# Both masked attentions in the turned form, with a quad's values in three pieces

## The reference, cut to what matters

```python
x = x + L0_xattn(layernorm(x), ctx, ctx, mask0, ...)      # first attention, masked
x = x + L0_ffn(layernorm(x), ...)                         # its weights are quantised to -1, 0, 1
...
x = x + L3_xattn(layernorm(x), ctx, ctx, mask3, ...)      # fourth layer's attention, masked
x = x + L3_ffn(layernorm(x), ...)

# L0_xattn and L3_xattn, B = 4, 16 heads of 8, 256 queries, 1601 keys
q, k, v = heads(Q @ Wq.T + bq), heads(K @ Wk.T + bk), heads(V @ Wv.T + bv)
scores = q @ k.T / sqrt(8)
scores = scores + mask0 * -1e9                  # L0: float mask, 1 is masked
scores = where(mask3 == 0, -1e9, scores)        # L3: int mask, 0 is masked
out = (softmax(scores) @ v).reshape(...) @ Wo.T + bo
```

## Time and profile before

| | before |
|---|---|
| median of three runs | 2109.28 us (2107.88 to 2111.71) |
| the profiled execution | 2111.81 us |
| its span, first to last instruction | 2110.0 us |
| mean granted clock of TensorE | 0.941 |
| TensorE matmuls | busy 1899.7 us, 90% |
| TensorE weight loads | busy 1336.2 us, 63% |
| VectorE | busy 1334.4 us, 63% |
| ScalarE | busy 1297.4 us, 61% |
| GpSimd | busy 309.7 us, 15% |
| DMA | 87.69 MB, mean 42 GB/s |

### The profile page before, as it was taken

One profiled execution on the slowest core, in us unless ns is written; L12 is line 12 of the kernel. 1 busy time (PEld: TensorE's weight loads), 2 busy tenths in 40 slices (PEclk: granted clock), 3 DMA queues, 4 the chain that ended last, 5 costly groups with the idle time before them and its releaser, 6 DMA issues. The chain is left out here.

```text
span 2110.0 us, 43468 instructions
## 1 busy us (share of the span) xinstructions
PE 1899.7 (90%) x16932; PEld 1336.2 (63%) x16935; DVE 1334.4 (63%) x3286; ACT 1297.4 (61%) x2097; POOL 309.7 (15%) x475
## 2 busy tenths in 40 slices
PE   6999999967868659999999999999995799999997
PEld 4777777735634637777777777777774456666553
DVE  7888888877455244555555555555555877777773
ACT  5999999955356125555555555555564466666664
POOL 4000000000122110000000000000000445555552
PEclk9999999977877679999999999999997799999998
DMA  7211111102260510000000000000000621111110
GB/s 239 58 43 47 42 47 43 42 16 77 48 187 18 150 36 2 1 1 1 1 2 1 1 1 2 1 1 1 1 2 1 210 57 42 47 43 47 47 37 17
DMA packets 55307, 87.69 MB, mean 42 GB/s; under 512 B 9881, under 2 KB 31437, under 8 KB 55105
## 3 DMA queue, kind: packets, MB, share of 16 engines
q1 hardware_dynamic: 54593, 83.87, 13.5%
q0 software_dynamic: 512, 1.05, 0.2%
HBM read 66.93 MB, written 17.96 MB: 40 GB/s over the span
## 5 line engine op out<-in xcount | busy, mean ns | idle before, releaser
L2528 ACT ACTIVATE a_prT<-bank 128x512 f32<-128x512 f32 (+1 forms) x448 | 232.8, 565 | 328.2 <-PE bank L2437 328.0
L1226 DVE CUSTOM_DVE_ANT_0 a_attn_junk<-wide,a_mask 128x801 f32<-128x801 f32 (+1 forms) x256 | 246.1, 990 | 92.0 <-PE wide L1023 91.2
L2583 DVE CUSTOM_DVE_ANT_0 a_sc<-wide,a_zeros 128x1024 f32<-128x1024 f32 (+1 forms) x256 | 243.1, 987 | 87.3 <-PE wide L2423 87.3
L1149 ACT ACTIVATE a_attn_prT<-bank 128x512 f32<-128x512 f32 (+1 forms) x378 | 196.9, 567 | 106.6 <-PE bank L1043 103.5
L1554 DVE CUSTOM_DVE_ANT_0 a_attn_sc<-wide,a_mask 128x801 f32<-128x801 f32 (+1 forms) x256 | 252.9, 988 | 12.3 <-PE wide L1401 10.6
L1417 PE MATMUL bank<-ident,a_attn_sc 128*128 128x128 f32 x1664 | 244.8, 276 | 14.9 <-ACT a_attn_prT L1511 13.8
L1417 PEld LDWEIGHTS bank<-ident,a_attn_sc 128*128 128x128 f32 x1664 | 199.0, 142 | 62.3 <-issue 42.3
L2437 PE MATMUL bank<-ident,a_sc 128*128 128x128 f32 x1664 | 231.3, 277 | 1.5 <-ACT a_prT L2528 1.5
L2437 PEld LDWEIGHTS bank<-ident,a_sc 128*128 128x128 f32 x1664 | 185.1, 140 | 54.4 <-issue 28.1
L1517 ACT ACTIVATE a_attn_sc<-a_attn_sc,a_attn_nmx 128x1601 f32<-128x1601 f32 x128 | 209.6, 1637 | 3.0 <-DVE a_attn_nmx L1560 3.0
L2489 PEld LDWEIGHTS bank<-a_prT,a_vt 128*64 128x64 f32 x3328 | 180.3, 137 | 48.4 <-issue 47.0
(11 more groups left out here) (476 smaller groups left out, 3089.8 us busy)
## 6 DMA issues: line engine op xcount, KB each, us to landing
a_ks<-a_k_parts SPq DMA_DIRECT2D x384, 75.0 KB
a_k_parts<-a_proj_kp SPq DMA_DIRECT2D x18, 416.0 KB, 4.9
a_qx<-a_q_stack SPq DMA_DIRECT2D x384, 12.0 KB
moe_w1b<-in_e_w SPq DMA_DIRECT2D x15, 256.0 KB, 3.0
ctxT<-in_ctxT SPq DMA_DIRECT2D x4, 832.0 KB, 6.5
a_ctxn<-in_ctxn SPq DMA_DIRECT2D x4, 832.0 KB, 7.1
a_k_parts<-a_last_slot SPq DMA_DIRECT2D x6, 416.0 KB, 4.1
m_q_stack<-m_proj_qp SPq DMA_DIRECT2D x9, 256.0 KB, 3.5
```

The source lines that it names most:

```text
L1149: act.activation(probs(u)[0:keys, kt:kt + m, :], bank_of(s, f"W{g}")[0:keys, 0:m * S].rearrange("p (t q) -> p t q", q=S), ACT.Exp).then_in ...
L1226: dve.tensor_tensor_reduce(junk[:, n % 2, 0:w], S_WIDE[n % 2][:, 0:w], mask(qt, at, w), 1.0, LOWEST, ALU.add, ALU.max, mx[:, p % 2, qt, e, ...
L2528: copy = lambda out, src: act.activation(out, src, ACT.Copy)
L2583: dve.tensor_tensor_reduce(sc[:, s % 2, h, at:at + w], S_WIDE[h][:, 0:w], zeros[:, 0:w], 1.0, LOWEST, ALU.add, ALU.max, mx[:, s % 2, h, p: ...
```

## The change

In `quad_attention_stage`:

- The pieces of the values are 5, 4 and 4 key tiles (40, 32 and 32 products' records) instead of 7 and 6, in steps 4q + 7, 4q + 8 and 4q + 9. In a step the piece now stands behind T0 and P0 instead of ahead of them.
- The third piece has the row that ScalarE's copy of the sums, their turn and the normalisation go by, so these move one step on, and `batch_end` moves from 21 + 16b to 22 + 16b. The loop has 72 steps instead of 71.
- Each piece counts on `pv_done`, and an exponential that reuses a slot waits for the piece that last read its key tiles, group by group, instead of for the whole quad at the first group.
- The stage can carry the quantisation of weights: their load when turned groups of unit 61 are done; the product of ones in the last step (71), and VectorE's part in step 70, behind the last normalisation and ahead of the moments and the last batch's addition.

`row_quad_stage` is removed, and the first attention goes through `quad_attention_stage`. For it `masked_head_layer` now also makes `cap` and `maskT`, has a ring of 6, loads a transposed mask (`mask0T`, float, padded to 1664 keys) and the three paddings. These go to SP's queue at the head of `project_stage` (the contexts and the mask stay ahead of the layernorm stage). In both attentions the paddings count on `k_stored[0]`, so they are waited for ahead of the first operands' loads, and the conversions are regrouped: `maskT` whole in block 1; the two halves of `cap` and one half of `mask` in block 2; the other half in block 3.

```diff
 def quad_attention_stage(core, name, ..., last_prT, weights=None):
-    CHUNKS = [(0, 7), (7, KT)]
+    CHUNKS = [(0, 5), (5, 9), (9, KT)]
-    LAST = UNITS + TURN + 4
+    LAST = UNITS + TURN + 5
...
         def batch_end(s):
-            b = (s - 21) // 16
-            return b if s >= 21 and (s - 21) % 16 == 0 and b < B else None
+            b = (s - 22) // 16
+            return b if s >= 22 and (s - 22) % 16 == 0 and b < B else None
+        def chunks_before(kt):
+            return sum(first < kt for first, last in CHUNKS)
...
+            if weights:
+                sp.wait_ge(turned, NG * (UNITS - 2))
+                sp.dma_start(weights[0], weights[1]).then_inc(w_in, 16)
...
-                if last == KT:        
-                    ins.then_inc(pv_done, 1)
+                ins.then_inc(pv_done, 1)
...
+            def sum_weights():
+                pe.wait_ge(w_chain, 1)
+                pe.wait_ge(drained, 4 * UNITS)
+                pe.matmul(S_WIDE[0][:, 0:3], core.ones[:, :], part[:, :], start=True, stop=True).then_inc(w_chain, 1)
...
-                values(s)
+                if s == LAST - 1 and weights:
+                    sum_weights()
                 turned_group(s, 0)
                 score_piece(s, 0)
+                values(s)
                 turned_group(s, 1)
...
-                    if u >= PRT:
-                        act.wait_ge(pv_done, (u - PRT) // 4 + 1)
+                if u >= PRT:
+                    act.wait_ge(pv_done, len(CHUNKS) * ((u - PRT) // 4) + chunks_before(kt + m))
...
+            def quantise_weights():
+                raw, raw_dram, wq, mean = weights
+                link = Link(dve, w_chain)
+                dve.wait_ge(w_in, 16)
+                link(dve.tensor_reduce(part[:, :], raw, X, ALU.add, apply_absolute_value=True))
+                link.n += 1
+                dve.wait_ge(w_chain, link.n)
+                link(dve.tensor_scalar(mean, S_WIDE[0][:, 0:3], 1.0 / (FF0 * D), 1e-5, ALU.mult, ALU.max))
+                link(dve.reciprocal(inv[:, :], mean))
+                for i in range(3):
+                    ins = dve.tensor_scalar(raw[:, i, :], raw[:, i, :], inv[:, i:i + 1], ROUND, ALU.mult, ALU.add)
+                link(ins)
+                link(dve.tensor_scalar(raw, raw, ROUND, 1.0, ALU.subtract, ALU.min))
+                link(dve.tensor_scalar(wq, raw, -1.0, None, ALU.max))
...
                 maximum(s, 3)
+                if s == LAST - 2 and weights:
+                    quantise_weights()
                 if batch_end(s) is not None:
...
-def row_quad_stage(...):
...
 def project_stage(...):
-            sp.wait_ge(k_stored[0], 16 * (3 + len(k_rows(0))))
+            sp.wait_ge(k_stored[0], 16 * (3 + len(k_rows(0)) + sum(sem is k_stored[0] for _, _, sem in ahead)))
...
 def masked_head_layer(...):
-    STACK, RING, LAST_ROW = 72, 6 if replaced else 4, MAX_ROW + 6
+    STACK, RING, LAST_ROW = 72, 6, MAX_ROW + 6
...
+                later = [(seenT[:, :, :], inp["mask0T"].rearrange("(t p) q -> p t q", p=P), mask_in)] + pads
...
+            mask_work = [[], [conversion(maskT[:, :, :], seenT[:, CAPPED_TILES:, :], is_masked, MASKED, first=True)],
+                         [conversion(cap[:, 0:2, :], seenT[:, 0:2, :], is_valid, CAP),
+                          conversion(cap[:, 2:4, :], seenT[:, 2:4, :], is_valid, 1.0),
+                          conversion(mask[:, 0, :], seen[:, 0, :], is_masked, MASKED)],
+                         [conversion(mask[:, 1, :], seen[:, 1, :], is_masked, MASKED)]]
```

362 lines of the change are left out of this document (31 added, 331 removed).

## The result

| | before | after |
|---|---|---|
| median | 2110.12 us of five runs (2107.88 to 2113.66) | 2119.78 us of five runs (2117.29 to 2126.93) |
| ratio, 95% interval | | 1.0057 (1.0044 to 1.0070) |
| the profiled execution | 2111.81 us, span 2110.0 | 2126.93 us, span 2125.2 |

What follows compares the result with a forecast made beforehand. Chains through VectorE's maxima and GpSimd, not summed busy time, were taken to set the pace. 0.5 + 1.3 + 6.1 + 2.4 = +10.3 on 2111.8 gives 2122.1 us, or 2119.6 against the median; range 2094 to 2136.

Steps and rivals of the forecast that it cites:

- The quad: Both attentions, first value piece to the next quad's: 24.36 us against 24.28; taken as +0.08, between -1.7 and +0.5.
- P0 behind the first piece: Score piece after the 40-product value piece: waits on a VectorE maximum, 0.4 us.
- the turn of the sums: After the quad's third value piece: TensorE waits 0.4 us for ScalarE's copy, then 0.36 of work.
- V32 to V32: Leg from second to third value piece: chain through VectorE's maxima gives 6.15 us, TensorE alone 6.07.
- V40 to V32: Leg from first to second value piece: 6.58 us by the chain through VectorE's maxima and cap, TensorE alone 6.21.
- Rival 1: Not slower: waits on the maxima vanish, TensorE near 22.6; quad 22.6 to 23.8, total 2084 at 23.1; 20%.
- Rival 2: GpSimd's second masked-weights instruction under the cap takes 1.57, not 1.16; first piece waits 0.4 longer per quad, 2131; 13%.
- Part 1: Values in three pieces, both attentions: +0.5 us, bounds -24 and +8, with 0.86 gained at the end.
- Part 2: First attention in the turned form: swap by itself +0.8 us, +1.3 with the +0.5 of Part 1.
- Part 3: Weights' quantisation at the first attention's end, on VectorE behind the last normalisation: +6.1 us, bounds 5 and 7.
- Part 4: First projection: added mask and padding loads and VectorE conversions, +2.4 us, bounds 1.9 and 5; fourth layer 0.
- rival 3: First projection: first keys land behind contexts, mask, its transpose and paddings; +5 instead of +2.4, total 2122; 5%.

Runs made afterwards that it cites:

- the reordered kernel: Changed kernel with VectorE's cap placed by step, normalisation behind the last maximum, TensorE's turn of the sums later in its step: quad 23.83, 2104.3 us in one run.
- the quantisation early: Changed kernel with VectorE's weight quantisation called in step 66 and the product of ones ahead of step 68's values: 2115.3 us, ratio to before 1.0026.
- the conversions late: Changed kernel with the first attention's mask and cap conversions one block later (blocks 2 and 3): 34.42 us to first score product, 2119.4 us in one run.
- the paddings later: Changed kernel with the three paddings issued behind the first block's key stores: 32.71 us to first score product, 2116.4 us in one run.
- the kernel with the fourth layer alone: Kernel before with the changed quad_attention_stage in the fourth layer only, first attention left in row form: 2109.2 us, ratio 0.9999.

## Why the prediction was right, and where it was not

**The quad** was worked out as 24.36 us and is 24.38. Its legs were 5.87 + 5.76 = 11.63, 6.58 and 6.15, and are 11.58, 6.59 and 6.21. The two larger waits that I named are in the trace: P0 behind the first piece (0.23 shown, 0.38 of occupied time beyond its neighbours) and the turn of the sums (0.27); there is no wait for a probability slot. The waits of 0.1 behind the other two pieces are not there. The two hundredths are better than the working deserves: the errors of the legs are up to 0.06 and partly cancel, and one leg has the right length for a wrong reason. V32 to V32 was worked out as a chain of 6.15 over TensorE's own 6.07; it is 6.21 with the cap in the chain and without it, so it is TensorE's own work, priced 0.14 too low. In V40 to V32 the chain is real: doubling the cap gave back its length whole, and taking the cap out cut the leg by 0.28.

**Rival 1** (the waits vanish, TensorE near its own time) did not come. It came in part only when the cap, the normalisation and the sums' turn were moved, to 23.50. **Rival 2** (GpSimd stretched under the cap) did not come either: in the changed kernel the second masked-weights instruction of the light step takes 1.16, clear of the cap. But its mechanism is real: it is what kept the reordered kernel at 23.83.

**Part 1 in the fourth layer** was +0.5 and is -0.17 in the trace and 0.9999 timed. The quads give +1.0 of the 1.4 expected (from the first piece to that of the last quad but one 341.98 us against 341.01; the batch ends cost nothing), and the end, from the first piece of the last quad but one to the last normalisation, gives back 0.26 and not 0.86 (28.49 against 28.75). That alone would be +0.7; the first steps were 0.85 shorter, at a granted clock of 0.63 instead of 0.60 over their first 23 us, which is scatter between executions.

**Part 2, the swap**, was +1.3, with the quantisation 7.4, and the attention measures 408.3 to 416.4, so 8.1. The 0.7 that is missing is the end: from the first piece of the last quad but one to the last normalisation it takes 28.74 us here, as before (28.75), so of the 0.86 that I had counted as gained there nothing came. The start, 37.24 us to the first piece, is 0.3 longer than the 36.96 of the row that it was taken from (the granted clock is at 0.50 to 0.52 until 71.7), and the quads are 0.25 below what I gave them; that is within the scatter of the start, 35.9 to 37.5 in three more kernels with the same order there (the quantisation early, the conversions late, the paddings later).

**Part 3, the quantisation**, was +6.1 and is 5.9 (7.86 against 1.95 us), for the reason given. What I did not see is the 9.5 us in which VectorE idles ahead of that normalisation; the same work fits there.

**Part 4, the projection**, is the term that failed: +2.4, measured +4.15. In eight executions with the changed code first query product to first score product takes 34.8 to 36.0 us; with the code of before it took 31.18 and, in the kernel with the fourth layer alone, 32.27, so the term is 2.5 to 4.9. The size is inside my bounds of 1.9 and 5, the mechanism is not the one that I took. I priced 2304 columns at 3.96 us, from int32 rows in pieces of 768, and took 2.3 of it; they take 1.36. By the two elements a cycle of the Trainium skill (VectorE: DVE Perf Modes, section Mode 2×_2P) it would be an estimated 1.2, and the trace is near that rule.

The row was also read wrong. The prediction put its 1.32 against the rule down to int32, but the timeline of before shows what it is:

```profile
1668.32 1.23 POOL L1726 TENSOR_TENSOR a_proj_kp<-a_proj_rest,a_proj_kp 128x416 bf16<-128x416 f32 x1 [0.17 <-ACT a_proj_kp L1703]
1668.64 1.32 DVE L1831 TENSOR_SCALAR a_maskT<-a_seenT 128x768 bf16<-128x768 int32 x1
```

Such a piece starts under a GpSimd instruction and ends 0.41 us behind it, so some 0.9 of its 1.32 is standing beside GpSimd, once a piece. In the changed kernel the fourth layer converts its 2304 int32 columns in one piece beside GpSimd in 1.84 us, and the float columns took 1.91 beside it with the conversions late: the type is not the reason. The 3.96 counted three times what is lost once a piece.

The loss is instead a wait of 3.44 us for the transposed mask, held up by the paddings' transfers. I had the 2.35 MB of transfers only as part of an upper bound and in rival 3, and placed them at the first keys' landing; it is the conversion in block 1 that meets them. The overpriced conversion and the unseen wait nearly made up for each other.

The total came within 0.2 us of the forecast. With 0.5, 1.3, 6.1 and 2.4 against -0.2, 2.2, 5.9 and 4.15 in the profiled executions, where the terms add up to 12.1 and the medians show 9.7, that closeness is partly luck; the sign and the place of the loss are not.

The Trainium skill's rule on the most-contended engine (Perfetto Trace Analysis, section Identifying the Most-Contended Engine) would have made rival 1 the likelier one, by TensorE's weight loads busy 57 of 97.7 us. The trace doesn't bear that out here: moving TensorE's pieces alone left the quad at 24.38, two of its three legs stand at or within 0.3 us of TensorE's own pace, and a new order on VectorE, with the turn of the sums moved too, brought 0.88 us of a quad.

## What to carry to other kernels

When a wait in front of an engine's long piece is hidden by moving the piece, look for the chain that produced the wait: here it ran on from VectorE's maxima, and the wait only changed its name until the order on VectorE was changed. To see whether such a chain sets the pace, make it both longer and shorter: longer alone can overtake the engine that had set it. Before taking a short instruction out of a chain, list who waits for its result in each step of the pattern; one place for all four steps cost 37 us, a place by step, with the normalisation and the turn of the sums moved too, gained 15 in the first try, against the changed kernel. Work that is tied to no one belongs where its engine idles, and transfers that nobody waits for yet belong behind the one that somebody waits for. Before a row's time is multiplied, look at what ran beside it.

## What the runs showed of the hardware

VectorE's cap and GpSimd's instructions, all on SBUF, held each other up. A GpSimd instruction that started under the cap took 0.59 instead of 0.21 us or 2.01 instead of 1.49, as the earlier trace rows had shown with 1.57 instead of 1.16; the one that was under way when the cap started kept its 1.49. The cap that came beside GpSimd's second masked-weights instruction took 1.6 us instead of 0.6. The maxima, which read their scores from PSUM, took 0.99 beside any of them. VectorE's conversions did the same: 768 columns took 1.32 us under a GpSimd instruction and ended 0.41 behind it. Which property of the instructions decides this was not tested by itself.

The same DMA engines, fully busy in both cases, moved 147 GB/s with the paddings in the queue and 417 GB/s in the same three microseconds without them. A 1024 B packet of the transposed mask took 51 ns ahead of the paddings and 141 ns beside them.
